# Taking the reversed sum of delta from the projection's PSUM bank instead of from SBUF

## The reference

```python
x_dbl = xc @ W_x
delta, Bm, Cm = jnp.split(x_dbl, [DT_RANK, DT_RANK + N], axis=-1)
delta = jax.nn.softplus(delta @ W_dt + b_dt)
...
dA = jnp.einsum('bld,dn->bldn', delta, A)
dB_u = jnp.einsum('bld,bld,bln->bldn', delta, u, B)
dA_shift = jnp.concatenate([dA[:, 1:], jnp.zeros_like(dA[:, :1])], axis=1)
dA_cumsum = jnp.exp(jnp.cumsum(dA_shift[:, ::-1], axis=1)[:, ::-1])
xs = jnp.cumsum(dB_u * dA_cumsum, axis=1) / (dA_cumsum + 1e-12)
y = jnp.einsum('bldn,bln->bld', xs, C)
```

## Time and profile before

| what | value |
|---|---|
| median of 3 runs | 544.12 us (543.4 to 544.31) |
| the profiled execution | 544.86 us, of which span 543.0 us |
| DVE busy | 415.1 us (76%) |
| PE busy | 409.1 us (75%) |
| POOL busy | 373.5 us (69%) |
| ACT busy | 349.2 us (64%) |
| loop, first scan to the end of the last | 129.12 us to 499.73 us |

### The profile page before, as it was taken

One profiled execution on the slowest core, in us unless ns is written; L12 is line 12 of the kernel. 1 busy time (PEld: TensorE's weight loads), 2 busy tenths in 40 slices (PEclk: granted clock), 3 DMA queues, 4 the chain that ended last, 5 costly groups with the idle time before them and its releaser, 6 DMA issues.

```text
span 543.0 us, 5369 instructions
## 1 busy us (share of the span) xinstructions
PE 409.1 (75%) x1588; PEld 233.1 (43%) x1588; DVE 415.1 (76%) x513; ACT 349.2 (64%) x627; POOL 373.5 (69%) x290
## 2 busy tenths in 40 slices
PE   5999996877975959996577799867656854857664
PEld 1336664544532425563243456534323632423533
DVE  3242556234899999899999989799899899798543
ACT  1135444228678669678489869968966866992362
POOL 2025630017869889799879999987799999977410
PEclk9999999686989779997988899787878989986966
DMA  8900000047000037200003440000244000000000
GB/s 312 233 1 1 2 0 2 0 160 308 1 4 1 1 116 264 85 4 0 2 0 143 164 159 4 11 12 0 116 174 174 2 22 1 1 1 0 7 16 22
DMA packets 10414, 34.30 MB, mean 63 GB/s; under 512 B 2208, under 2 KB 5104, under 8 KB 10160
## 3 DMA queue, kind: packets, MB, share of 16 engines
q1 hardware_dynamic: 9984, 33.17, 17.5%
q10 hardware_dynamic: 400, 0.79, 0.4%
HBM read 32.57 MB, written 1.38 MB: 63 GB/s over the span
## 4 chain that ended last, share of the span: by engine, by line
POOL 30%; DVE 12%; issue 11%; ACT 11%; PE 9%; ACTq 0%; DVEq 0%; POOLq 0%
POOL big L455 14%; POOL big L461 9%; DVE PS L1291 5%; PE PS L583 4%; ACT PS L994 3%; ACT big L1003 3%; PE PS L808 3%; POOL big L499 2%; DVE big L1300 1%; PE PS L732 1%; DVE big L1306 1%; ACT L994 1%; ACT big L1045 1%; DVE big L1384 1%; PE PS L787 1%
## 5 line engine op out<-in xcount | busy, mean ns | idle before, releaser
L808 PE MATMUL PS<-big,eighth 128*128 128x384 f32 x384 | 172.1, 587 | 69.3 <-POOL big L461 68.7
L1291 DVE TENSOR_TENSOR_SCAN PS<-PS,big 128x768 f32<-128x768 f32 x96 | 168.5, 1755 | 17.2 <-ACT PS L994 14.8
L455 POOL TENSOR_TENSOR big<-big,bc 128x768 f32<-128x768 f32 x96 | 173.4, 1820 | 0.0
L808 PEld LDWEIGHTS PS<-big,eighth 128*128 128x128 f32 x384 | 83.2, 227 | 140.7 <-POOL big L461 88.5
L461 POOL TENSOR_TENSOR big<-big,bc 128x768 f32<-128x768 f32 x60 | 109.2, 1821 | 39.7 <-DVE big L1300 39.5
L994 ACT ACTIVATE PS<-big,Aneg 128x384 f32<-128x384 f32 x192 | 103.7, 572 | 41.7 <-DVE big L1306 28.4
L1003 ACT ACTIVATE big<-big,guard,Ahalf 128x380 f32<-128x380 f32 x192 | 122.2, 690 | 0.0
L1300 DVE SCALAR_TENSOR_TENSOR big<-big,PS 128x768 f32<-128x768 f32 x60 | 57.0, 950 | 5.8 <-ACT big L1003 0.5
L420 POOL TENSOR_TENSOR big<-bc,cst_sb 96x1536 f32<-96x1536 f32 x8 | 22.0, 2752 | 43.3 <-ACT bc L903 32.2
L583 PE MATMUL PS<-big,w_in_sb 96*128 96x384 f32 x96 | 43.8, 597 | 5.0 <-DVE big L1252 4.4
L583 PE MATMUL PS<-big 128*64 128x34 f32 (+3 forms) x416 | 43.7, 282 | 0.0
(11 more groups left out here) (151 smaller groups left out, 538.8 us busy)
## 6 DMA issues: line engine op xcount, KB each, us to landing
bc<-bc_rows SPq DMA_DIRECT2D x32, 768.0 KB, 4.3
bc<-in_x_cols_dram SPq DMA_DIRECT2D x3, 512.0 KB, 6.5
bc<-in_x_cols_dram SPq DMA_DIRECT2D x1, 1536.0 KB, 8.7
out_dram<-h SPq DMA_DIRECT2D x4, 288.0 KB, 2.7
big<-in_f_in_dram SPq DMA_DIRECT2D x1, 768.0 KB, 10.8
bc<-in_cw_dram ACTq DMA_DIRECT2D x1, 576.0 KB, 5.6
w_in_sb<-in_w_in_dram SPq DMA_DIRECT2D x1, 576.0 KB, 14.4
big<-in_f_out_dram SPq DMA_DIRECT2D x1, 384.0 KB, 11.9
```

Source lines behind the costliest of these rows:

```text
L455: P.tensor_tensor(pair(vR[:, g % VRING]), part(du, q, m).unsqueeze(1).broadcast_to([128, PAIR, QT]), rows_of(g, 0), ALU.mult).then_inc(sem ...
L808: ins = pe.matmul(y_sum, eighth[:, :], vR[:, g % VRING, QT * e:QT * (e + 1)], start=False, stop=True, skip_group_check=True)
L1291: V.tensor_tensor_scan(h_, h_, vR[:, g % VRING], 0.0, ALU.mult, ALU.add).then_inc(sem("scan_done"), 1)
```

## The change

`softplus` writes its result back into the projection's bank (from PSUM to PSUM, in place) and raises a new semaphore `softplus`. A new function `delta_out` on ACT waits for it, copies the bank to `delta` in SBUF and raises `delta_here`; for quarter 0 the two alternate, for the others come three softplus and then three copies. `sum_later` takes its second input from the bank and waits for `delta_here`; it raises `left_dt`, which now means that the bank is free. `times_u` waits for `delta_here`. In the tables the sums of quarters 1 to 3 move to the two steps behind `sp`, and the z stages of quarters 2 and 3 by one step.

```diff
-             dt0=-19, dt1=-19, dt2=-19, sp=-18, times_u=-16, later0=-14, later1=-11, later2=-9, edges=-6,
-             z0=-16, z1=-15, z2=-14, tz0=-15, tz1=-14, tz2=-13, zs0=-14, zs1=-13, zs2=-12)
+             dt0=-19, dt1=-19, dt2=-19, sp=-18, times_u=-16, later0=-17, later1=-17, later2=-16, edges=-6,
+             z0=-15, z1=-14, z2=-13, tz0=-14, tz1=-13, tz2=-12, zs0=-13, zs1=-12, zs2=-11)
...
-                   times_u=11, later0=12, later1=14, later2=17, edges=19, z0=12, z1=13, z2=14, tz0=13, tz1=14, tz2=15,
+                   times_u=11, later0=10, later1=10, later2=11, edges=19, z0=12, z1=13, z2=14, tz0=13, tz1=14, tz2=15,
...
-    LAST_READ.update({"xi%d" % i: "tap%d" % i, "cv%d" % i: "us%d" % i, "z%d" % i: "zs%d" % i, "dt%d" % i: "sp", "out%d" % i: "add%d" % i,
+    LAST_READ.update({"xi%d" % i: "tap%d" % i, "cv%d" % i: "us%d" % i, "z%d" % i: "zs%d" % i, "dt%d" % i: "later%d" % i, "out%d" % i: "add%d" % i,
...
             def times_u(q, m=slice(0, CT)):
-                job_left(pool, "dt", q, m if q == 0 else CT - 1)
+                pool.wait_ge(sem("delta_here"), CT * q + (m if q == 0 else CT - 1) + 1)
...
             def softplus(q, m):
                 job_here(act, "dt", q, m)
-                A.activation(part(delta, q, m), job_bank("dt", q, m)[:, 0:QT], ACT.Softplus, bias=bdt[:, m:m + 1]
-                             ).then_inc(sem("left_dt"), 1)
+                at = job_bank("dt", q, m)[:, 0:QT]
+                A.activation(at, at, ACT.Softplus, bias=bdt[:, m:m + 1]).then_inc(sem("softplus"), 1)
+
+            def delta_out(q, m):
+                act.wait_ge(sem("softplus"), CT * q + m + 1)
+                A.activation(part(delta, q, m), job_bank("dt", q, m)[:, 0:QT], ACT.Copy).then_inc(sem("delta_here"), 1)
...
             for m in range(CT):
                 softplus(0, m)
+                delta_out(0, m)
...
             def sum_later(q, m):
-                job_left(dve, "dt", q, m)
-                V.tensor_tensor_scan(part(later, q, m)[:, ::-1], keep[:, ::-1], part(delta, q, m)[:, ::-1],
-                                     0.0, ALU.mult, ALU.add).then_inc(sem("later_ready"), 1)
+
+                dve.wait_ge(sem("delta_here"), CT * q + m + 1)
+                V.tensor_tensor_scan(part(later, q, m)[:, ::-1], keep[:, ::-1], job_bank("dt", q, m)[:, 0:QT][:, ::-1],
+                                     0.0, ALU.mult, ALU.add).then_inc(sem("left_dt"), 1)
```

More of the change, by code:

```diff
@@ L94, in due @@
     return [q for q in range(NQ) if AT.get((name, q)) == g]
-SCALAR_WORK = dict(xn=4, turned=2, tap0=1, tap1=1, tap2=1, tu0=1, tu1=1, tu2=1, tz0=1, tz1=1, tz2=1, x_out=1, sp=6,
+SCALAR_WORK = dict(xn=4, turned=2, tap0=1, tap1=1, tap2=1, tu0=1, tu1=1, tu2=1, tz0=1, tz1=1, tz2=1, x_out=1, sp=9,
                    quant_in=4, q1_out=2, silu=6, square0=1, square1=1,
@@ L435, in times_u @@
             def times_u(q, m=slice(0, CT)):
-                job_left(pool, "dt", q, m if q == 0 else CT - 1)
+                pool.wait_ge(sem("delta_here"), CT * q + (m if q == 0 else CT - 1) + 1)
                 P.tensor_tensor(part(du, q, m), part(delta, q, m), part(u, q, m), ALU.mult).then_inc(sem("du_ready"), 1)
             def edges(q, m):
-                pool.wait_ge(sem("later_ready"), CT * q + m + 1)
+                pool.wait_ge(sem("left_dt"), CT * q + m + 1)
                 pool.wait_ge(sem("du_ready"), delta_of(q, m))
@@ L999, in guards @@
                 if j == 0:
-                    act.wait_ge(sem("later_ready"), CT * q + m + 1)
+                    act.wait_ge(sem("left_dt"), CT * q + m + 1)
                 lt = part(later, q, m).rearrange("p (b l) -> p b l", b=QB)
@@ L1073, in beside @@
                         softplus(q, m)
+                    for m in range(CT):
+                        delta_out(q, m)
                 for q in due("quant_in", g):
```

## The result

The changed kernel takes 555.04 us in the median (551.22 to 556.07, 4 runs), the one before 544.21 us beside it (543.4 to 548.06, 4 runs). The ratio is 1.0146 with a 95% interval of 1.0097 to 1.0194: slower, by 5 to 11 us (the medians lie at the far end of that, 10.8 us apart). 547.4 us was predicted, with a range that ended at 551.0; the sign was right, the size was not. The profiled execution took 555.91 us, of which span 554.1, so 11.1 us more than the one of before (span 543.0).

What follows compares the result with a forecast made beforehand. No one engine was taken as the bound; DVE and POOL hand the end to each other. Start +8.5, quarters -2.8, -3.4, +1.0 make +3.3: 548.2 us profiled, 547.4 median (0.74 lower), range 543.0 to 551.0.

Steps and rivals of the forecast that it cites:

- Removed: DVE's twelve sums: with delta in the bank each takes 0.93 us anywhere, so DVE loses 10.0 us.
- rival 4: Sums still wait for POOL because keep and output stay in SBUF; gains of 6.2 us go, 553.6 us; chance 0.05.
- The start: From the delta projections to scan 5: held banks make PE and ACT wait in turn; scan 5 8.5 us late.
- rival 1: Start runs at full PE clock or with smaller gaps: 4.9 us late instead of 8.5, 543.8 us; chance 0.15.
- rival 3: PE's clock stays at half through the first `cv`, making the start 11.7 and the time 550.6 us; chance 0.15.
- Quarter 1: Scan 5 to quarter 2's start: DVE's excess is 2.9 us, POOL can follow into its gaps; -2.8 us.
- ACT's extra work falls beside the two sums: Quarter 1, step 10: ACT's copies, 1.45 us in one piece, hide beside 1.75 us of DVE sums.
- Quarter 2: Sums at steps 31 and 32: of 5.4 us excess, two POOL gaps of 1.74 us go; -3.4 us.
- The gain there is nothing: Quarter 2, up to 262.40: sums delay step 31's guard 1.7 us, POOL arrives as before without idling 1.74 us; gain 0.
- Quarter 3: Steps 53 to 56 onward: scan 56 3.4 us later, partly regained as later sums go; +1.0 us, ends 0 and +2.
- Rival 2: DVE alone bounds: all 10.0 us come back; with the start at 4.9, 541.8 us, even 540.5; chance 0.13.
- upper ends, +12.2: Each term at its slow end: 11.7 - 1.5 - 0 + 2 = +12.2 us, but not all at once.

Runs made afterwards that it cites:

- e7_keep_moved: The e4_keep_psum kernel with the sums of quarters 1 to 3 and the z stages at the change's steps; 542.17 us, ratio 0.9913.
- e9_sums_first: The change with the sums of blocks 1 and 2 of quarter 0 also done before the loop; 545.93 us, ratio 0.9987.
- e1_start_old: The change with quarter 0 kept the old way, quarters 1 to 3 as changed; 545.19 us, ratio 0.998.
- e11_behind_guard: The e9_sums_first kernel with the sums of quarters 1 to 3 behind their step's guard instead of ahead of it; 544.17 us, ratio 0.9961.
- e4_keep_psum: The kernel before with only the ones (keep) moved to PSUM, each sum two scans of 192; 536.36 us, ratio 0.9793.
- e13_behind_q3_old: The e11_behind_guard kernel with quarter 3 as before, except its sums stand behind their guards; 541.37 us, ratio 0.9937.
- e2_start_q3_old: The change in quarters 1 and 2 only; quarters 0 and 3 the old way, with old steps in quarter 3; 541.16 us, ratio 0.9889.
- e3_start_new: The kernel before with the change in quarter 0 alone, all tables and quarters 1 to 3 old; 555.31 us, ratio 1.015.

## Why the prediction was wrong

**Removed: right.** Every sum is between 918 and 953 ns; `later` and `keep` in SBUF make no difference, and rival 4 falls. By the Trainium skill (SBUF — State Buffer, "Who interferes with whom") a DVE instruction with at most one SBUF input stays clear of GpSimd; these twelve rows agree.

**The start: right in its mechanism, 0.8 short.** +9.3 instead of +8.5. The three `xi`, which had run in one piece,

```profile
126.74 7.02 PE L583 MATMUL PS<-big,w_in_sb 96*128 96x384 f32 x12 [0.58 <-ACT big L940]
```

now stand apart, and the rows of PE follow the reckoning link by link:

```profile
121.71 1.62 PE L583 MATMUL PS<-big,w_dt_sb 48*128 48x384 f32 x2 [3.04 <-DVE big L1291]
...
127.69 0.88 PE L709 MATMUL PS<-cst_sb,big 96*96 96x96 f32 x4 [0.57 <-ACT big L940]
129.23 2.90 PE L583 MATMUL PS<-big,w_in_sb 96*128 96x384 f32 x4 [0.67 <-ACT big L940]
...
135.43 2.90 PE L583 MATMUL PS<-big,w_in_sb 96*128 96x384 f32 x4 [3.29 <-ACT big L952]
139.00 2.90 PE L583 MATMUL PS<-big,w_in_sb 96*128 96x384 f32 x4 [0.67 <-ACT big L952]
...
144.72 0.81 PE L729 MATMUL PS<-ones,diagW 128*128 128x384 f32 x2
```

The first `cv` stands at 144.72; counted from the first projection it is 8.6 us later than before (8.0 predicted). The clock was 0.56 from 135 to 145 us, so rival 1 falls, and the two `cv` passes took 0.81 us as before, so rival 3 does too. Nearly all of the 0.8 us is the first row: I took that projection at the 0.91 us of the earlier trace rows, but it ran at the lower clock behind its wait, in 1.62.

**Quarter 1: wrong, 0.0 instead of -2.8.** The step that failed is "POOL idles 1.59 us for a guard at 188.75 and in such a gap again some 13 us on, so it can follow". The gap was looked for behind the sums, where they had stood; but they now stand at step 10, ahead of another guard. For quarter 2 I made just this argument (the two sums "hold the guard of step 31 back"), and for quarter 1 I did not. After, POOL and DVE show it:

```profile
181.22 1.81 POOL L461 TENSOR_TENSOR big<-big,bc 128x768 f32<-128x768 f32 x1 [2.33 <-DVE big L1308]
...
195.32 0.56 DVE L1269 SCALAR_TENSOR_TENSOR big<-big,PS 128x384 f32<-128x384 f32 x1 [0.98 <-ACT big L964]
```

POOL waits 2.33 us, more than the 1.12 of `e7_keep_moved`, since DVE itself had waited for ACT (0.83 us before the first sum): the projections of delta ran at the lower clock here, six passes in 4.21 us, where they take 2.20 before and in the kernels with an early start. Of the 2.8 us missing, 1.2 to 1.8 go with the place of the sums (behind an early start `e9_sums_first` has -1.6 and `e1_start_old` -1.0, and `e11_behind_guard` -2.9), and the other 1.0 to 1.6 are lost only behind the late start. "ACT's extra work falls beside the two sums" is therefore wrong in detail: ACT's piece was 6.5 us long (172.7 to 179.3) against 2.8, but most of the difference is PE's clock (2.4 us of waiting between the softplus), and where the start is early the copies add nothing with the sums right behind them.

**Quarter 2: wrong, -0.7 instead of -3.4.** That the two sums hold the guard of step 31 back held: POOL waits 1.45 us there (1.7 predicted). "The gain there is nothing" did not: against before, DVE's scans were 9.8 us late at step 31 and only 6.7 at step 35, so 3.1 us were in hand. What failed for the total is "Behind it, DVE is ahead and the two gaps of 1.74 us before 275.42 and 282.52 go": the scans were 8.6 us late at step 36, 6.7 at 40, and 9.1 from 43 on.

```profile
258.70 1.81 POOL L461 TENSOR_TENSOR big<-big,bc 128x768 f32<-128x768 f32 x1 [1.45 <-DVE big L1308]
...
273.86 0.49 ACT L964 ACTIVATE big<-PS 128x384 f32<-128x384 f32 x1 [5.48 <-PE PS L583]
...
274.46 0.56 DVE L1269 SCALAR_TENSOR_TENSOR big<-big,PS 128x384 f32<-128x384 f32 x1 [1.37 <-ACT big L964]
...
294.92 1.76 DVE L1299 TENSOR_TENSOR_SCAN PS<-PS,big 128x768 f32<-128x768 f32 x1 [1.56 <-ACT PS L998]
...
303.08 1.82 POOL L461 TENSOR_TENSOR big<-big,bc 128x768 f32<-128x768 f32 x1 [2.55 <-DVE big L1308]
```

The late guard, with the z stages a step later, made a late z tanh as in quarter 1, here with 5.48 us of idling on ACT; DVE lost 1.37 us at it and 1.56 at a later scan, and POOL's gaps only moved. In `e11_behind_guard`, with the sums behind the guards and the z stages as here, the wait of 1.37 us is gone. I followed the shift as far as POOL and no further, to PE, ACT and back to DVE.

**Quarter 3: right in its mechanism, +2.0 instead of +1.0.** Scan 56 came 3.3 us later (3.4 predicted), and 3.0 of it were back by scan 64; but then the scan of step 65 waited 3.00 us for ACT where it had waited 1.53, and 0.5 more went by step 68. The term that was too small is "the silu chain on ACT carries 1.0 of it on": it measured 2.0.

**Sum.** 0.8 at the start, 2.8, 2.7 and 1.0 in the quarters, and 0.5 before the loop are 7.8 us; 548.2 + 7.8 = 556.0, and the profiled execution took 555.91. Rival 2 is half right, which the change hides: most of the sums' waiting does come back (7.8 to 9.3 us in `e4_keep_psum`), but it needed "the start at 4.9", and the moved steps took the gain away. The prediction's own upper ends, +12.2, would have reached the measured time; the range stopped at 551.0 because they were taken not to come "all at once". Three did: quarter 1 went past its end, quarter 2 came near its end of 0, quarter 3 stood at its end of +2.

## What to carry to other kernels

An operation that is moved to an earlier step has a place in its queue as well as a step: look at what stands right behind it and who waits for that, and follow the delay through every engine until it comes back to the first. When an evacuation turns into a late last reader of a bank, the price is in the bank table, not in the operation; move that reader to where its engine idles before paying for it, or get the second input out of SBUF in another way, as here by putting the constant operand into spare PSUM columns.

## What the runs showed of the hardware

Which of the two waits, a scan with both inputs in SBUF or a product of POOL, depends on how they meet. In `e13_behind_q3_old` the three sums of quarter 3 read both inputs from SBUF at the old steps, but stand behind the guards, and none was longer than the bare price. Durations (ns min/median/max, first and last start us), then the first of them with POOL's product beside it:

```profile
L1320 DVE TENSOR_TENSOR_SCAN big<-keep,big x3: 951/952/953, 354.4 to 373.9; 128x384 f32<-128x384 f32 x3
```

```profile
354.43 0.95 DVE L1320 TENSOR_TENSOR_SCAN big<-keep,big 128x384 f32<-128x384 f32 x1
...
354.59 2.40 POOL L480 TENSOR_TENSOR big<-big,bc 128x768 f32<-128x768 f32 x1 [0.42 <-DVE big L1337]
```

The product began 0.16 us behind the sum and took 2.40 us instead of 1.81; at the other two it is 2.38 and 2.40. The wait had changed sides. Ahead of their guards, as in `e2_start_q3_old`, the same three sums took 2.55, 2.03 and 0.93 us. Before, both sides paid once: a product of POOL took 2.48 us at 175.17, beside DVE's sum of 2.81.

```profile
175.17 2.48 POOL L461 TENSOR_TENSOR big<-big,bc 128x768 f32<-128x768 f32 x1
```

Such a wait can be longer than one POOL instruction, and no semaphore is in it: the sum of 5.23 us from 256.25 on the earlier trace rows was still running when POOL had ended one product and done two more, which began after the sum had:

```profile
257.09 3.57 POOL L455 TENSOR_TENSOR big<-big,bc 128x768 f32<-128x768 f32 x2
```

So besides the waits at semaphores there are waits inside an instruction, which a profile shows as a long duration and not as idle time.

PE's clock after a pause was not decided by the pause alone: the z projection above is one case, and behind the same wait of 3.04 us the third projection of delta ran in 1.62 us in the change and in 0.88 in `e9_sums_first` and `e3_start_new`. With the granted clock at 0.50 or 1.00, chains through PE differ by a microsecond or two (1.7 us at scan 41 above). What decides between the two is not shown. Splitting a scan in two cost 0.05 us (0.98 for both halves in `e4_keep_psum` against 0.93).
